# Self attention: two neighbouring P tiles per GpSimd remainder, and key scores eight units ahead

## What is computed

```python
half = num_heads // 2
base = 24.0 ** (1.0 / half)
slopes = (1.0 / base ** jnp.arange(1, half + 1, dtype=dtype))[:, None, None]
fwd = slopes * jnp.tril(rel) + jnp.triu(neg, 1)
bwd = slopes * jnp.triu(-rel) + jnp.tril(neg, -1)
...
scores = jnp.einsum('bhqd,bhkd->bhqk', q, k) * (1.0 / np.sqrt(hd)) + bias[None]
attn = jax.nn.softmax(scores, axis=-1)
out = jnp.einsum('bhqk,bhkd->bhqd', attn, v)
```

## Time and profile before

| | us |
|---|---|
| median of 3 runs | 3126.95 (3123.92 to 3128.47) |
| the profiled execution | 3123.28 |
| its span | 3121.1 |
| PE / DVE / ACT / POOL busy | 2634.2 / 2318.2 / 1762.4 / 1874.1 |
| self attention's remainders on GpSimd | 577.0 in 512 instructions |
| cross attention's remainders on GpSimd | 906.6 in 448 instructions |

### The profile page before, as it was taken

How to read it: one execution, slowest core, us unless ns; L and a number is a source line. 1 busy time by engine, 2 the same in 40 slices (tenths; PEclk the granted TensorE clock), 3 DMA queues, 4 the chain that set the end, 5 groups by cost and what they waited for, 6 DMA issues and landing times. The chain is left out here.

```text
span 3121.1 us, 77095 instructions
## 1 busy us (share of the span) xinstructions
PE 2634.2 (84%) x24119; PEld 1431.1 (46%) x24119; DVE 2318.2 (74%) x4525; ACT 1762.4 (56%) x3255; POOL 1874.1 (60%) x1424
## 2 busy tenths in 40 slices
PE   7999478888886869999999999980999899703999
PEld 3555235555554534555555555550444344301444
DVE  8888667777775767888888888867333467697776
ACT  3444257777775435666666666654233477696333
POOL 3444479999997317999999999996100144300000
PEclk9999779999998988999999999995999999856999
DMA  8999724444445662222122131115644588797332
GB/s 305 336 334 342 267 96 134 136 126 131 135 133 169 235 202 60 53 75 66 51 80 62 49 98 50 47 54 172 214 153 158 200 278 281 258 415 282 110 126 81
DMA packets 320920, 511.28 MB, mean 164 GB/s; under 512 B 35669, under 2 KB 155221, under 8 KB 320810
## 3 DMA queue, kind: packets, MB, share of 16 engines
q1 hardware_dynamic: 317674, 503.65, 48.3%
q0 software_dynamic: 1952, 6.29, 0.6%
q10 hardware_dynamic: 1184, 0.01, 0.0%
HBM read 270.95 MB, written 194.28 MB: 149 GB/s over the span
## 5 line engine op out<-in xcount | busy, mean ns | idle before, releaser
L1102 POOL TENSOR_TENSOR cross_plo<-cross_p 128x1024 f16<-128x1024 f32 x448 | 906.6, 2058 | 73.4 <-ACT cross_p L940 69.7
L940 ACT ACTIVATE cross_p<-cross_st 128x512 f32<-128x512 f32 x1024 | 556.2, 595 | 289.1 <-PE cross_st L874 289.0
L1015 DVE CUSTOM_DVE_ANT_0 cross_junk<-cross_sc,rows 128x1024 bf16<-128x1024 f32 x512 | 619.0, 1219 | 110.5 <-PE cross_sc L835 98.2
L1102 POOL TENSOR_TENSOR self_plo<-self_p 128x1024 f16<-128x1024 f32 (+7 forms) x512 | 577.0, 1165 | 19.1 <-ACT self_p L940 18.8
L940 ACT ACTIVATE self_p<-self_st,self_strip 128x512 f32<-128x512 f32 (+3 forms) x768 | 415.3, 582 | 148.0 <-PE self_st L872 116.8
L1015 DVE CUSTOM_DVE_ANT_0 self_junk<-self_sc,self_strip 128x1024 bf16<-128x1024 f32 (+7 forms) x512 | 371.1, 752 | 140.8 <-PE self_sc L835 136.0
L869 PE MATMUL cross_st<-cross_qa,cross_ka 97*128 97x512 f16 x1024 | 390.4, 381 | 2.5 <-ACT cross_p L940 1.7
L874 PE MATMUL cross_st<-rows,idbig 128*128 128x512 f16 x1024 | 389.9, 381 | 0.0
L835 PE MATMUL cross_sc<-cross_ka,cross_qa 96*128 96x512 f16 x1024 | 311.3, 386 | 22.3 <-DMA cross_ka<-scr_k_hi 16.7
L897 PEld LDWEIGHTS cross_o<-cross_vh,cross_p 128*128 128x128 bf16 x4096 | 270.1, 97 | 75.0 <-issue 21.7
L897 PE MATMUL cross_o<-cross_vh,cross_p 128*128 128x65 f16 x4096 | 297.4, 191 | 4.6 <-POOL cross_plo L1102 4.2
(11 more groups left out here) (254 smaller groups left out, 5710.3 us busy)
## 6 DMA issues: line engine op xcount, KB each, us to landing
self_strip<-self_strips SPq DMA_DIRECT2D x68, 516.0 KB, 3.2
scr_gate<-gt_y SPq DMA_DIRECT2D x96, 256.0 KB, 2.1
v_w<-scr_gate SPq DMA_DIRECT2D x96, 256.0 KB, 4.1
scr_h<-v_w SPq DMA_DIRECT2D x96, 256.0 KB, 4.0
j_h<-scr_h SPq DMA_DIRECT2D x48, 512.0 KB, 9.6
d_o<-scr_o SPq DMA_DIRECT2D x9, 1536.0 KB
scr_up<-v_y SPq DMA_DIRECT2D x48, 256.0 KB, 4.3
j_u<-scr_up SPq DMA_DIRECT2D x24, 512.0 KB, 12.0
```

Of the source, the lines that this page charges most:

```text
L940: nc.scalar.activation(p32[u % NPR][:, q0:q1], stp[cc % 2][:, 0:q1 - q0], ACT.Exp, bias=bias, scale=SM).then_inc(expd, 1)
L1015: nc.vector.tensor_tensor_reduce(junk[slot % 2][:, 0:w], sc[slot % 2][:, 0:w], bias, 1.0, -3e38, ALU.add, ALU.max, qmax[n % 2][:, qt:qt + ...
L1102: nc.gpsimd.tensor_tensor(plo[u % NPR][:, q], p32[u % NPR][:, q], high[:, q], ALU.subtract).then_inc(lo_g, 1)
```

## The change

In the self attention the P tiles of two neighbouring units lie side by side in one buffer of 1024 + 128 = 1152 columns (the widths of a pair always add up to that), eight such buffers for p32 and for plo, so 16 slots in place of 8. GpSimd makes both remainders with one instruction, when the second unit's exponentials are done; low of the first unit of a pair does nothing. P·V of either unit waits for that one instruction. The leads become 21 for scores and 8 for key scores, from 19 and 6. The cross attention keeps 19, 6 and 8 slots, two to a buffer of 2048 columns, with one instruction per unit.

```diff
-SLEAD = 19
-ELEAD = 6
-NPR = 8
+PAIR = 2
@@ attention_phase
+        SLEAD, ELEAD, NPP = (21, 8, 8) if causal else (19, 6, 4)
+        NPR = PAIR * NPP
+        PW = S + P if causal else PAIR * S
-        p32 = [sb(f"p32_{j}", [P, S], F32) for j in range(NPR)]
-        plo = [sb(f"plo{j}", [P, S], F16) for j in range(NPR)]
+        p32 = [sb(f"p32_{j}", [P, PW], F32) for j in range(NPP)]
+        plo = [sb(f"plo{j}", [P, PW], F16) for j in range(NPP)]
+        def width(u):
+            n, k, kt = keys_of(u)
+            a, z = query_range(n, kt)
+            return z - a
+        def spot(u):
+            return u // PAIR % NPP, 0 if u % PAIR == 0 else (width(u - 1) if causal else S)
+        def high_of(u):
+            j, b = spot(u)
+            return p32[j][:, b:b + width(u)].bitcast(BF16).rearrange("p (q h) -> p q h", h=2)[:, :, 1]
+        def lows_of(u):
+            j, b = spot(u)
+            if on_vector(u) or causal and u % PAIR == 0 and not on_vector(u + 1):
+                return None
+            if causal and u % PAIR == 1 and not on_vector(u - 1):
+                return j, 0, b + width(u)
+            return j, b, b + width(u)
+        def lows_by(u, vector):
+            if vector:
+                return sum(on_vector(m) for m in range(u + 1))
+            return sum(lows_of(m) is not None for m in range(u + 1)) + (lows_of(u) is None)
@@ values, TensorE
-                        pe.wait_ge(lo_g, i * LG + lows_before(u, False) + 1)
+                        pe.wait_ge(lo_g, i * LG + lows_by(u, False))
+                    j, b = spot(u)
+                    high, rest = high_of(u), plo[j][:, b:b + width(u)]
@@ exps, ScalarE
-                        nc.scalar.activation(p32[u % NPR][:, q0:q1], stp[cc % 2][:, 0:q1 - q0], ACT.Exp,
+                        nc.scalar.activation(p32[j][:, b + q0 - a:b + q1 - a], stp[cc % 2][:, 0:q1 - q0], ACT.Exp,
@@ low, GpSimd
-                    if on_vector(u):
+                    if lows_of(u) is None:
                         return
                     pool.wait_ge(expd, i * CS + chunks_by(u) + 2)
-                    nc.gpsimd.tensor_tensor(plo[u % NPR][:, q], p32[u % NPR][:, q], high[:, q], ALU.subtract).then_inc(lo_g, 1)
+                    j, a, z = lows_of(u)
+                    high = p32[j][:, a:z].bitcast(BF16).rearrange("p (q h) -> p q h", h=2)[:, :, 1]
+                    nc.gpsimd.tensor_tensor(plo[j][:, a:z], p32[j][:, a:z], high, ALU.subtract).then_inc(lo_g, 1)
```

More of the change, by code:

```diff
@@ L677, in on_vector @@
             return not causal and u % UH == 4
-        def lows_before(u, vector):
-            return sum(on_vector(m) == vector for m in range(u))
-        LV, LG = lows_before(HB * UH, True), lows_before(HB * UH, False)
+        def width(u):
[18 more added lines that the diff above has]
+            return sum(lows_of(m) is not None for m in range(u + 1)) + (lows_of(u) is None)
+        LV, LG = lows_by(HB * UH - 1, True), sum(lows_of(m) is not None for m in range(HB * UH))
         def within(last, u):
@@ L885, in values @@
                     if on_vector(u):
-                        pe.wait_ge(lo_v, i * LV + lows_before(u, True) + 1)
+                        pe.wait_ge(lo_v, i * LV + lows_by(u, True))
                     else:
-                        pe.wait_ge(lo_g, i * LG + lows_before(u, False) + 1)
+                        pe.wait_ge(lo_g, i * LG + lows_by(u, False))
                     a, z = query_range(n, kt)
-                    high = p32[u % NPR][:].bitcast(BF16).rearrange("p (q h) -> p q h", h=2)[:, :, 1]
+                    j, b = spot(u)
+                    high, rest = high_of(u), plo[j][:, b:b + width(u)]
                     for qt in range(a // P, z // P):
-                        q = slice(qt * P, (qt + 1) * P)
+                        q = slice(qt * P - a, qt * P - a + P)
                         out = ob[qt // 4]
@@ L897, in values @@
                         nc.tensor.matmul(out[:, qt % 4, :], high[:, q], vh[n % NQK][:, kt, :], start=first, stop=False, skip_group_check=True)
-                        mm = nc.tensor.matmul(out[:, qt % 4, 0:HD + 1], plo[u % NPR][:, q], vh[n % NQK][:, kt, 0:HD + 1],
+                        mm = nc.tensor.matmul(out[:, qt % 4, 0:HD + 1], rest[:, q], vh[n % NQK][:, kt, 0:HD + 1],
                                               start=False, stop=last_kt, skip_group_check=True)
@@ L1026, in low @@
                     dve.wait_ge(expd, i * CS + chunks_by(u) + 2)
-                    q = slice(*query_range(n, kt))
-                    high = p32[u % NPR][:].bitcast(BF16).rearrange("p (q h) -> p q h", h=2)[:, :, 1]
-                    nc.vector.tensor_tensor(plo[u % NPR][:, q], p32[u % NPR][:, q], high[:, q], ALU.subtract).then_inc(lo_v, 1)
+                    j, b = spot(u)
+                    q = slice(b, b + width(u))
+                    nc.vector.tensor_tensor(plo[j][:, q], p32[j][:, q], high_of(u), ALU.subtract).then_inc(lo_v, 1)
                 def gather(i, n):
@@ L1095, in low @@
                 def low(i, u):
-                    n, at, kt = keys_of(u)
-                    if on_vector(u):
+                    if lows_of(u) is None:
                         return
                     pool.wait_ge(expd, i * CS + chunks_by(u) + 2)
-                    q = slice(*query_range(n, kt))
-                    high = p32[u % NPR][:].bitcast(BF16).rearrange("p (q h) -> p q h", h=2)[:, :, 1]
-                    nc.gpsimd.tensor_tensor(plo[u % NPR][:, q], p32[u % NPR][:, q], high[:, q], ALU.subtract).then_inc(lo_g, 1)
+                    j, a, z = lows_of(u)
+                    high = p32[j][:, a:z].bitcast(BF16).rearrange("p (q h) -> p q h", h=2)[:, :, 1]
+                    nc.gpsimd.tensor_tensor(plo[j][:, a:z], p32[j][:, a:z], high, ALU.subtract).then_inc(lo_g, 1)
                 def prologue():
```

## The result

The changed kernel took 3146.16 us (median of 7 runs, 3144.98 to 3166.36), the kernel before 3128.47 in the same rounds. The ratio over all runs is 1.0068 (that of the two medians 1.0057), with a 95% interval of 1.0039 to 1.0097: slower by 0.4 to 1.0%. Two of the seven runs lay 20 us above the other five; why is open. The profiled execution took 3144.98 us with a span of 3142.5, so the span grew by 21.4 us. The cross attention did not change: from its first to its last P·V matmul it took 903.15 us before and 903.14 after.

The account below looks back on a forecast made before the run. GpSimd was taken to hold the self attention's loop at 9.0 us a head, through VectorE's scaling waiting for its instruction's end. Steady heads +21 and ends +0.5, called +22 us, on the 3126.95 median gave 3149 us, range 3116 to 3163.

Parts of the forecast that it names:

- What bounds the kernel: Self attention's steady loop: GpSimd sets the pace, 9.0 us a head, through VectorE's scaling ending 0.28 us after its instruction.
- A pair at 2.10 us: GpSimd's 1152 wide remainder in self attention: 2.10 us, from the line through the single widths.
- 1.89 and 2.88: Lower and upper limits in us for the 1152 wide remainder: the line at 1024, and GpSimd's slowest price per column.
- The head worked out: One self attention head followed step by step with the change: period up from 9.02 to 9.34 us, 9.37 with the branch.
- The pair's wait: P·V waiting for both units' exponentials and remainder: hidden by the 7.9 us that the lead of 8 gives.
- The ends: Start and end of self attention: 2.0 and 1.5 us added, about 3 given back, sum +0.5 us.
- The steady heads: Self attention's steady part: 60 heads, each 0.35 us longer, +21 us.
- A: Rival: the scaling misses the pair's instruction or the pair ends before it is due; heads 8.74 us, 3110 us; 17%.
- B: Rival: the pair starts about 0.35 us earlier, the scaling waits as before; heads 9.0 to 9.05, 3127 to 3130; 10%.
- C: Rival: the 1152 wide instruction is dear; 3161 us at 2.3 us, 3275 at 2.88; 7% together, the last 2%.

Follow-up runs that it names:

- the early scaling and a cut: The changed kernel with self attention's reciprocal and scaling moved right behind the 384 maximum, and pair 640 + 512 done as 768 and 384 columns: 3111.53 us.
- the cut: The changed kernel with each head's first pair (1024 + 128) done in two GpSimd instructions of 768 and 384 columns, signalled once at the end: 3118.71 us.

## Why the prediction was right

The predicted 3149 us stands against 3146.16 measured, well inside the forecast's own range of 3138 to 3160. In spans, 22 us were forecast and 21.4 measured; in medians of the same rounds the growth is 17.7.

1. What bounds the kernel: right. The prediction said that GpSimd holds the loop through the end of the instruction that the scaling falls into. Six kernels make pairs and keep the scaling's two inputs (the changed one and five of the runs). They differ by at most one GpSimd instruction a head, in the leads and in the scaling's place, and take from 3111 to 3177 us; what sets them apart is the length of that one wait and the place it has in VectorE's queue. With single remainders (two runs) the head stayed at GpSimd's 9.02 us. One reading beside it was incomplete: between the two longest waits named, 116.4 and 102.6 us, lies a third, VectorE's for the scores, 114.0 us; it changes nothing in the argument.

2. A pair at 2.10 us: measured 2.11. The mean of 2.151 has the instruction behind the scaling in it, 2.29 us, which is held up for 0.18. Neither bound, 1.89 and 2.88, was needed. This float32 minus bfloat16 costs 1.83 ns per column at 1152 columns. The Trainium skill's "GPSIMD Engine Reference", section "Performance versus the Vector engine", has 4497 ns for 2048 columns, 2.2 ns per column, and the estimate by it, 2.53 us, lies 20% above the row.

3. The head worked out: P·V 1024 at 1.76 (measured 659.07 − 657.38 = 1.69), the pair from 3.24 to 5.34 (3.19 to 5.30), the scaling due at 4.6 (4.59) and over at 5.62 (5.58), scores 896 at 6.83 (6.78), the next head at 9.34 (9.34). The mean of 9.37 was 9.358. This was possible because the steps' durations and latencies were taken from the trace and the method had first been run on a head whose answer was known. The remark that TensorE alone would be at the next head at about the same time isn't borne out: TensorE is busy for 7.5 to 7.7 us a head in all these kernels, and with the early scaling and a cut most heads take 8.52 to 8.68 us.

4. The pair's wait: hidden, as said. In the changed kernel P·V starts 4.48 us or more after its remainder ended, and the runs with a cut keep that wait and are the fastest.

5. The ends were mis-sized in both parts: the first P·V came 4.4 us later (3.5 said), the end gave back some 2.4 (3 said), so +2 where the sum had +0.5. The steady heads brought 58 × 0.335 = 19.4 where 60 × 0.35 = 21 was said. The two errors, 1.5 each way, cancel; that the sum came out within 0.1 us of the span's growth is luck.

6. The rivals. A, the scaling outside a long instruction, did not happen by itself, but the cut brought it about: its price was put at 8.74 us a head, and the run shows 8.78 and 8.80 away from the loop's branch. What it left out is 0.08 us a head on the mean, lost next to that branch; GpSimd is nearly full again in this run (508.8 of 520 us), which may be why it isn't made up, but no run shows it. B and C did not occur.

## What to carry to other kernels

Where an instruction of one engine waits for the end of another's, as VectorE's scaling does here for GpSimd's, the length of the one is a latency of the other: merging small GpSimd instructions saves their fixed cost (0.14 us each here, the 0.396 of the 128 wide one less 0.2135 for its columns and 0.04 of overlap) and can lose more than that at a VectorE instruction behind which a queue stands. Look where each VectorE instruction that reads SBUF alone ends against the ends of GpSimd's instructions; a constant distance betrays the wait, which no view of waits shows, since it is recorded as duration. Then move that instruction to where its engine has room, or put a GpSimd boundary just before it is due.

## What the runs showed of the hardware that was not expected

An instruction with a single float32 input in SBUF waits too. The prediction named two inputs alone, and the expectation of the run left it open. In 10 heads in a row it ended 0.149 to 0.151 us after GpSimd's instruction, and the two-input form 0.28 us after. Alone, behind the last P·V, it takes 0.29 us and the two-input form 0.42, the same 0.13 us less. The Trainium skill has this in "Advanced Engine Details and Errata", section "GPSIMD Details": the conflict is with VectorE instructions in a 2-port performance mode or with two SBUF inputs. By that rule, the trace agrees, if this tensor_scalar ran in such a mode; its shorter time fits that, but no record names the mode. The maxima (one input in PSUM, one in SBUF) do not wait: 1.21 to 1.23 us for 1024 columns in all of these runs, under GpSimd's instructions, and 1.22 to 1.23 as well for the two of each run that no GpSimd instruction overlaps.

GpSimd pays as well: the 1152 wide instruction behind a scaling that waited takes 2.29 us and the others 2.11. Behind the one-input form it takes 2.16.

The longest wait in the changed kernel lies at its end, where the scores are over:

```profile
1003.71 2.10 POOL L1131 TENSOR_TENSOR self_plo<-self_p 128x1152 f16<-128x1152 f32 x1
1003.71 2.39 DVE L1079 TENSOR_TENSOR self_ost<-self_osum,self_rden 128x256 f32<-128x256 f32 x1
```

Here the scaling came just as the pair began, and took 2.39 us in place of the 0.42 that it needs alone.
